# A late place in each step for the gates' steps, picked sums and first norms; signatures in three parts

## The reference, cut to what matters

```python
x = x + attention(layernorm(x))        # 16 heads of 64, 4 key/value heads, 1024 keys, softmax
x = x + cross_attention(layernorm(x))  # 16 heads of 16 on 64 context rows per batch
x = x + ffn(layernorm(x))
# ffn: sigs = signs of signatures_raw at +-0.3 (64 tiles x 256); cluster_sigs = sign of the mean of each 8
#   cluster_gates = calibrate(xf @ cluster_sigs.T);  cluster = argmax          (8 clusters)
#   tile_gates    = calibrate(xf @ sigs.T);  tile = argmax within that cluster (8 tiles)
#   calibrate(s): f = 7 * sigmoid(s / temperature); interpolate 8 knots at f
#   h = gelu(xf @ w1 + b1); comp = tanh(h @ w2 + b2)                           (2 numbers per row)
#   mag = relu(comp @ spline_w1[tile] + b) @ spline_w2[tile] + b
#   y = layernorm(xf + mag * directions[tile] * output_scale) * gamma + beta
```

## Time and profile before

| | |
|---|---|
| median of three runs | 1867.39 us (1863.63 to 1867.97) |
| the profiled execution's own time | 1867.59 us |
| its span, first to last instruction | 1865.8 us |
| mean granted clock of TensorE | 0.983 |
| PE busy | 1753.6 us, 94% |
| DVE busy, ACT busy, POOL busy | 62%, 62%, 48% |

### The profile page before, as it was taken

One profiled execution on the slowest core, in us unless ns is written; L12 is line 12 of the kernel. 1 busy time (PEld: TensorE's weight loads), 2 busy tenths in 40 slices (PEclk: granted clock), 3 DMA queues, 4 the chain that ended last, 5 costly groups with the idle time before them and its releaser, 6 DMA issues.

```text
span 1865.8 us, 27544 instructions
## 1 busy us (share of the span) xinstructions
PE 1753.6 (94%) x9204; PEld 853.6 (46%) x9204; DVE 1156.6 (62%) x2783; ACT 1151.5 (62%) x1554; POOL 891.5 (48%) x811
## 2 busy tenths in 40 slices
PE   5899999999999999999999999999999999999994
PEld 3444454454544445454543445445454444544453
DVE  5465647566475774746657575665656767375757
ACT  3566756666566765666656765666657676566653
POOL 2445445545544544556545454545545465544620
PEclk9899999999999999999999999999999999999997
DMA  5200000100200000010110000001020000000000
GB/s 166 46 13 1 1 12 1 24 12 13 57 1 12 1 18 7 1 35 1 46 24 1 12 1 24 1 1 35 1 57 1 2 1 24 12 1 1 1 12 12
DMA packets 96606, 32.32 MB, mean 17 GB/s; under 512 B 76304, under 2 KB 90704, under 8 KB 96464
## 3 DMA queue, kind: packets, MB, share of 16 engines
q1 hardware_dynamic: 96464, 30.56, 7.8%
HBM read 13.48 MB, written 4.19 MB: 9 GB/s over the span
## 4 chain that ended last, share of the span: by engine, by line
PE 75%; DVE 10%; ACT 7%; issue 5%; POOL 2%; DMA 0%; ACTq 0%; DVEq 0%; POOLq 0%; SPq 0%
PE attended L1290 21%; PE key_scores L1271 19%; PE misc L1200 7%; PE misc L1330 5%; PE max_scores L1249 5%; PE misc L1300 3%; PE misc L1370 2%; DVE relu L1934 2%; ACT relu L1648 2%; PE misc L1361 1%; PE misc L1434 1%; ACT probs L1657 1%; PE misc L1423 1%; PE misc L1205 1%; DVE row_stat L2225 1%
## 5 line engine op out<-in xcount | busy, mean ns | idle before, releaser
L1657 ACT ACTIVATE probs<-key_scores 128x1024 f32<-128x1024 f32 x512 | 524.2, 1024 | 481.0 <-PE key_scores L1271 401.8
L2429 POOL TENSOR_TENSOR prob_sum<-prob_sum,probs 128x512 f32<-128x512 f32 x383 | 491.7, 1284 | 151.3 <-ACT probs L1657 128.7
L1290 PE MATMUL attended<-probs,values 128*64 128x512 f32 x2048 | 557.7, 617 | 0.1
L1934 DVE CUSTOM_DVE_ANT_0 relu<-max_scores,relu 128x512 f32<-128x512 f32 x508 | 330.2, 687 | 330.3 <-PE max_scores L1249 329.2
L1271 PE MATMUL key_scores<-q_high,k_chain 64*128 64x512 f32 x2048 | 460.4, 446 | 13.0 <-ACT probs L1657 12.0
L1271 PEld LDWEIGHTS key_scores<-q_high,k_chain 64*128 64x128 f32 x2048 | 192.8, 185 | 453.2 <-issue 240.2
L1954 DVE TENSOR_TENSOR running_sum<-running_sum,probs 128x512 f32<-128x512 f32 x384 | 266.3, 693 | 11.1 <-ACT probs L1657 3.1
L1648 ACT ACTIVATE relu<-max_scores 128x1024 f32<-128x1024 f32 x254 | 259.0, 1020 | 21.5 <-PE max_scores L1249 15.8
L2425 POOL TENSOR_TENSOR prob_sum<-probs 128x512 f32<-128x512 f32 x64 | 82.1, 1283 | 359.0 <-PE misc L1300 352.3
L1249 PE MATMUL max_scores<-k_max,q_high 64*128 64x512 f32 x1016 | 210.2, 409 | 27.2 <-DVE row_max L1934 19.2
L1271 PE MATMUL key_scores<-q_low,k_chain 64*128 64x512 f32 x1024 | 204.3, 395 | 0.0
(11 more groups left out here) (435 smaller groups left out, 1929.0 us busy)
## 6 DMA issues: line engine op xcount, KB each, us to landing
k_chain<-k_chain SPq DMA_DIRECT2D x32, 256.0 KB, 3.7
shift_row<-row_max SPq DMA_DIRECT2D x512, 0.5 KB, 2.0
buf_a<-in_x SPq DMA_DIRECT2D x8, 512.0 KB, 4.0
k_max<-k_max SPq DMA_DIRECT2D x16, 256.0 KB, 3.4
x_in<-in_x SPq DMA_DIRECT2D x7, 512.0 KB, 4.2
out_x<-buf_b SPq DMA_DIRECT2D x7, 512.0 KB, 3.0
heads_out<-in_qkv_wT SPq DMA_DIRECT2D x1, 1536.0 KB, 10.0
wo<-in_o_wT SPq DMA_DIRECT2D x1, 1024.0 KB, 6.6
```

The costliest lines, as they stand in the source:

```text
L1290: tensor.matmul(attended[head * HD:(head + 1) * HD, :], values_of(b, g // 2)[:, kt, g % 2 * HD:(g % 2 + 1) * HD], prob_slot(u, kt, head), ...
L1657: scalar.activation(probs[(u * KT + kt) % len(probs)][:, :, :], key_scores[:, :, :], ACT.Exp).then_inc(S["exp"])
L1934: vector.tensor_tensor_reduce(out=relu_of(u, i)[:, head, :], in0=max_area(u, i)[:, head, :], in1=relu_of(u, i)[:, head, :], scale=1.0, sca ...
L2429: gpsimd.tensor_tensor(prob_sum[1][:, :], prob_sum[1][:, :], probabilities, ALU.add).then_inc(S["prob_sum1"])
```

## The change

A fifth place, `AFTER`, is added at the end of each step, behind `scores` and `max_d` or `max_s`. Moved to it: `cal_b` of both calibrations (with the first also `tanh_b`), the first pair of the norms before cross-attention and before the ffn, the first pair of `x_norm`, and `tile_scores` with the `cal_a` behind it. `pick_tiles` now follows `first_max` at once, in the same step. The signatures' 12 instructions are cut into 5 (`sigs_a`) and 7 (`sigs_c`), and `sigs_c`, `sigs_b` and `knot_table` ask for `ROOM`.

By the planner's rules this gives, beyond the moves inside a step: in the odd tails `cal_exp` of the tiles moves from step 173 to 172 of 512 (and likewise 128 and more steps on), `cal_d` and `cal_e` to 173, `cal_g` from 175, an odd step, to 174, an even one, `first_max` from 177 to 175, and all behind it two steps earlier (`x3` from 188 and 189 to 186 and 187, with the chunk's store DMA from 189 to 187). In the even tails no piece changes its step but `pick_tiles`, `tile_scores` and `cal_a` (112 to 111). `x_prep` of chunk 2 moves from steps 17 to 21 to steps 23 to 27, with its `load_x` DMA of chunk 3 on SP from 21 to 27; `x_prep` of chunks 5 and 7 starts two steps earlier. The number of instructions is the same.

```diff
-EARLY_R, EARLY, LATE, ROOM = "early float32r", "early", "late", "late, where VectorE has room"
+EARLY_R, EARLY, LATE, ROOM, AFTER = "early float32r", "early", "late", "late, where VectorE has room", "behind all else of a step"
...
@@ x_prep
     for pair in range(NT // 2):
-        yield LATE
+        yield LATE if pair else AFTER
         plan.put("x_norm", t, pair)
...
@@ setup
     plan.put("sigs_a")
-    yield LATE
-    plan.put("sigs_b")
-    yield LATE
-    plan.put("knot_table")
+    for stage in ("sigs_c", "sigs_b", "knot_table"):
+        yield ROOM
+        plan.put(stage)
...
@@ calibration
     plan.put("cal_exp", j, which)
-    yield LATE
+    yield AFTER
     plan.put("cal_b", j, which)
...
@@ attention, the end of a step
             if second:
                 plan.put("max_rows", u, tile)
+        preps.go_on(0, AFTER)
+        background.go_on(0, AFTER)
         for lane in (units, preps, background):
             lane.tidy()
...
@@ sigs_a
                 vector.tensor_tensor(sig, raw_sig, diff, ALU.add).then_inc(S["sigs"])
-                dve.wait_ge(S["sigs"], n + 5)
+
+            def sigs_c():
+                by_tile = sig.rearrange("p k (c t) -> p k t c", c=CL)
+                n = before("sigs", "sigs_c")
+                dve.wait_ge(S["sigs"], n)
                 vector.tensor_tensor(total, by_tile[:, :, 0, :], by_tile[:, :, 1, :], ALU.add).then_inc(S["sigs"])
                 for i in range(2, TPC):
-                    dve.wait_ge(S["sigs"], n + 4 + i)
+                    dve.wait_ge(S["sigs"], n - 1 + i)
                     vector.tensor_tensor(total, total, by_tile[:, :, i, :], ALU.add).then_inc(S["sigs"])
```

More of the change, by code:

```diff
@@ L115 @@
     "k2": {"k2": 1}, "k2T": {"k2T": 1}, "v2": {"v2": 1}, "v2_block": {"v2_block": 2},
-    "sigs_a": {"sigs": 12}, "sigs_b": {"sigs": 3, "temp": 4},
+    "sigs_a": {"sigs": 5}, "sigs_c": {"sigs": 7}, "sigs_b": {"sigs": 3, "temp": 4},
     "out_proj": {"out_proj": 1}, "residual_bias": {"residual_bias": 1}, "x1": {"x1": 1, "bn_stats": 1},
@@ L1987, in sigs_a @@
                 tern, diff = main.c[:, :, TILES:2 * TILES], main.c[:, :, 2 * TILES:3 * TILES]
-                by_tile = sig.rearrange("p k (c t) -> p k t c", c=CL)
                 n = before("sigs", "sigs_a")
@@ L2359, in _ @@
                 "q_split": q_split, "max_s": max_s, "begin": begin, "add": add, "bq2": bq2_, "mask": mask,
-                "v2_block": v2_block_, "sigs_a": sigs_a, "sigs_b": sigs_b, "x1": x1, "stats": stats,
+                "v2_block": v2_block_, "sigs_a": sigs_a, "sigs_c": sigs_c, "sigs_b": sigs_b, "x1": x1, "stats": stats,
                 "soft2": soft2, "normal2": normal2, "x2": x2, "tanh_a": tanh_a, "tanh_b": tanh_b, "cal_a": cal_a,
```

## The result

| | before | changed |
|---|---|---|
| median | 1866.93 us | 1883.03 us (1880.53 to 1884.26, 4 runs) |
| the profiled execution's own time | 1867.59 us | 1884.26 us |
| its span | 1865.8 us | 1882.4 us |
| PE busy | 1753.6 us | 1761.8 us |
| PE idle (span less busy) | 112.2 us | 120.6 us |

The ratio is 1.0088 (1.007 to 1.0105): slower, by 16 us. I forecast +8.2 and a time of 1875.5. The measured 1883.0 lies within the whole range of 1861 to 1885, but not in the forecast's own of 1871 to 1880, and it is nearer to the slower rival's 1886 than to my number. The last three rows of the table give the reason at once: PE idles 8.4 us longer, which is the forecast's +8.2, and it is busy 8.2 us longer with the same 9204 matmuls, which is not in the sum.

A forecast was written before the change was run, and what follows sets the result against it. PE, busy 94%, was taken to bound the kernel, with its waits on other engines. The terms summed to +8.2: 1867.6 + 8.2 - 0.2 = 1875.6, predicted as 1875.5; own range 1871 to 1880, whole range 1861 to 1885.

The forecast's parts named there:

- the slower rival: Odd tails: new waits some 6 us apart bring half-clock stretches costing 3.2 each, about +10, 1886; chance 0.13.
- signatures: Early DVE work: with seven of 12 instructions moved later, PE's 2.60 us wait for row maxima shrinks; -2.45.
- first norms, 8 places: Seven tails and chunk 3's x: the pair moved behind ACT's exponential delays the transposes, +0.71 each, +5.7.
- second norms: Transposes later by 0.8 in tails 1 and 3, 0.4 in 5 and 6, even tails 0; +2.4 in all.
- gates and picked sums, odd tails: Four odd tails: waits of 0.92 and 1.41 won, but spent by a late `cal_g`; +1.3 a tail, +5.2.
- picked sums, even tails: Three even tails: `tile_scores` and `cal_a` ahead of a running sum start row maxima 0.25 later; +0.75.
- `x3`: Tails 1, 3 and 5: moved from step 188 to 186, its 1.13 us wait goes three times; -3.4.
- x of chunks 5 and 7: Norms of the later chunks' x: no cost, since their transposes stand behind a projection; 0.
- clock: PE's half-clock stretches, three before, 17.00 us together: no change in the sum, treated only in rivals.
- the even tails' stretches vanish: Rival: splitting the even tails' second-norm wait removes all three half-clock stretches, saving 8.0, to 1867.5; chance 0.16.
- new ones come in the odd tails: Rival: half-clock stretches costing 3.2 each in three or four odd tails, about +10, 1886; chance 0.13.
- One of my own signs of being wrong: Changed kernel's timeline: the forecast is wrong if the half-clock stretches are fewer than three or more.

The follow-up runs named there:

- after_filled: The changed kernel with idle zero-adding matmuls on PE in 11 waits (four of 2.5 us, seven second norms'): 1873.36 us, ratio to before 1.0033.
- no_norms: The changed kernel with the first pairs of all norms and of `x_norm` back in their late place: 1871.81 us, ratio to before 1.0025.
- cal_only: Before, with only `cal_b` of both calibrations (and `tanh_b`) moved behind the row maxima: 1869.44 us, ratio to before 1.0009.

## Why the prediction was right, and where it was not

By its own steps, from the profiled executions (us):

| step | predicted | measured |
|---|---|---|
| signatures | -2.45 | -3.1 (2.60, and 0.47 behind them) |
| first norms, 8 places | +5.7 | +5.3 (0.66 each) |
| second norms | +2.4 | +4.0 |
| gates and picked sums, odd tails | +5.2 | +4.8 (3.53 - 2.33, four times) |
| picked sums, even tails | +0.75 | 0 (0.74 stays 0.74) |
| `x3` | -3.4 | -3.4 |
| x of chunks 5 and 7 | 0 | +0.4 |
| sum | +8.2 | +8.0 of the +8.4 in idle time |
| clock | 0, as two rivals | PE busy +8.2 |

**The norms** went as argued: ACT's idle time before the exponential is the resource that the pair had used. What was mis-sized is the second norm. In tails 1 and 3 it cost 0.98 each, not 0.8, and in tails 5 and 6 about 0.73 each, where I took 0.4, the middle of the bounds: there the upper bound of 0.8 would have been nearer. The three even tails, which I put at 0, cost 0.5 together, nearly all of it in tail 2. The wait before the scores did not go, as I had written: 0.8 of it stayed, and only the sum of the two waits came out as predicted.

**The odd tails** came out at the predicted total with two unseen terms, which cancel. From `pick_tiles` to PE the chain took 632.97 - 621.77 = 11.2, not 10.6. The first instruction of `cal_b` explains it. All 14 took 0.17 before; in the changed kernel

```profile
L2276 DVE TENSOR_SCALAR buf_c<-buf_c x14: 165/173/990, 395.7 to 1752.4; 128x32 f32<-128x32 f32 x14
```

(minimum, median, maximum in ns), and the four of about 990 are the tile gates' of the odd tails. At 625.53 it starts while POOL's sum of 625.19 runs to 626.48, and it ends with it. With the rule of the Trainium skill that the prediction weighed ("SBUF — State Buffer", section "Who interferes with whom"), that the one of the two engines which comes second is held up for the whole instruction of the other, this trace agrees. It cost 4 x 0.82 = 3.3 of chain, where I allowed up to 5.1 and left it out. What hid it has the other sign. The last instruction of `first_max` for the clusters, which took 0.93 in the earlier trace rows and ended with a POOL sum too, took 0.19 in the changed kernel, so `pick_tiles` began sooner: at 621.77, which is 622.85 in before's time (the second norm's transposes start 1.08 earlier in the changed kernel, 597.27 against 598.35), and I had 623.4. 0.55 sooner and 0.6 longer put PE at 634.05 in before's time, where I had 634.0; that is luck. The waits on the way were not divided as I had it either: twice 0.5 before the scores and 2.52 before the maxima, not 1.3 and 1 to 2.

**The step that failed** is the treatment of the clock. The sum holds it at 0. I had it only as two rivals, each whole: the even tails' stretches vanish (-8.0), or new ones come in the odd tails (+10). Both happened in part: 17.00 us of half clock behind the even tails became 6.80, and 23.80 us of new ones came, 20.40 behind the four waits of 2.5 us and 3.40 behind one of 1.45. Together they are an estimated +6.2 of PE's +8.2; about 2 us of its busy time I can't place, and the runs of one kernel differ by that much too. after_filled shows that it is a cost beside the waits.

One of my own signs of being wrong came true with it: the half-clock stretches are seven, not three. With the 6.2 the sum would be 14.4, against 16.7 measured in the profiled execution, but that is hindsight. My rows could not have given it: the 1.7 us waits had been followed by a fall three times out of three, the 2.60 us wait of the earlier trace rows had not. What they could give is that new waits of 1.3 to 2 us might cost clock, so that 0 was the wrong middle. That the measured time lies within the range at all is owed to its upper end, which the slower rival set.

**Left open:** why some waits are followed by a fall and others (1.74 for `q_low` at 587.09 and 2.60 at 109.12 in before) are not, and why the same wait is in one kernel and not in the next; and which order of gates would win. Four orders were tried besides the change's own, and each had its wait somewhere.

## What to carry to other kernels

Before work on an engine is moved out of a step's path, look at whether it ran in time that this engine had to idle in anyway; if so, moving it is a loss as soon as anything later on that engine is waited for. A chain that passes through several in-order engines can keep its wait when one piece is moved, and the wait only gets another releaser; so it was in each of the orders tried here. On TensorE a wait has two prices, its own length and the half clock that may follow; where a wait can't be removed, idle matmuls in it that end before it are worth trying.

## What the runs showed of the hardware

- The half clock after a wait: 0.92 and 1.41 us in the odd tails of before were never followed by one in its profile, those of 2.5 us were in four tails of four in the changed kernel and in no_norms, and filled with matmuls in none. The length does not settle it: the wait of 2.60 us at 109.12 of before was not followed by one, the same wait at 108.61 of cal_only was (granted clock 0.51 from 110.0 to 113.4), and the 1.7 us waits of the even tails were three times of three in before and once of three in no_norms. In 29 runs of before the time went with the mean clock: 1868.1 us on average at 0.983 (15 runs), 1866.6 at 0.985 (5 runs), 1862.16 in the one run at 0.988.
- A VectorE instruction of 0.17 us on 128x32 took 0.99 beside a GpSimd sum of 1.29, and ended with it, in four odd tails of four.
- An idle matmul of 128x512 took 18.7 / 71 = 0.26 us of PE.
